# Six edits to a one-core image kernel: three B banks in stage 1, early folds and sums, new banks for a step's last groups, and GpSimd adding the scaled output onto Y

## What is computed

```python
# layer 0: 4x4 mean pooling, two small attentions over the channels, bilinear upsampling, added to x
# layer 1: a Mamba block along one axis, 16 states, then a layernorm, added to x
def step(h, inps):
    dt_t, B_t, C_t, u_t = inps
    dA = jnp.exp(dt_t[..., None] * A)
    h = h * dA + dt_t[..., None] * B_t[:, None, :] * u_t[..., None]
    y = jnp.einsum('bds,bs->bd', h, C_t)
    return (h, y)
# layers 2 and 3: a Mamba-2 block along one axis, then along the other, twice each (8 calls),
# each with its projection added onto its input
scores = jnp.einsum('bln,bsn->bls', Cm, Bm)[..., None] * decay * dt[:, None, :, :]
y = _ssd(xh, dt, A, Bm, Cm) + rev(_ssd(rev(xh), rev(dt), A, rev(Bm), rev(Cm)))
y = _rmsnorm(y.reshape(b, l, DIN) * jax.nn.silu(z), gn_w)
```

## Time and profile before

| | us |
|---|---|
| median of 3 runs | 2561.96 |
| lowest and highest | 2560.93, 2566.42 |
| the profiled execution | 2571.92 |
| its span | 2570.1 |
| stage 0 | 0 to 126 |
| stage 1 | 126 to 863 |
| layernorm, folds, groupnorm | 863 to 910 |
| calls 0 to 3 | 910 to 1712 |
| X takes Y, groupnorm | 1712 to 1730 |
| calls 4 to 7 | 1730 to 2547 |
| the way out | 2547 to 2570 |

### The profile page before, as it was taken

How to read it: one execution, slowest core, us unless ns; L and a number is a source line. 1 busy time by engine, 2 the same in 40 slices (tenths; PEclk the granted TensorE clock), 3 DMA queues, 4 the chain that set the end, 5 groups by cost and what they waited for, 6 DMA issues and landing times.

```text
span 2570.1 us, 58820 instructions
## 1 busy us (share of the span) xinstructions
PE 1997.4 (78%) x24262; PEld 1009.7 (39%) x24262; DVE 1767.8 (69%) x2499; ACT 1666.5 (65%) x2730; POOL 1004.7 (39%) x794
## 2 busy tenths in 40 slices
PE   3257767676776569969969969967997997996996
PEld 3112222222222225535525535533553553553553
DVE  2578888888888867757666765666766665765664
ACT  1166767666676457857857757855875775775774
POOL 0034444444444505506515524522551550651452
PEclk6578888888788879989979989978989998997997
DMA  4000000000000011112112111102102201211111
GB/s 155 0 0 1 0 0 1 1 0 1 1 1 0 1 51 41 26 54 46 29 54 46 29 47 42 40 13 63 38 17 63 46 20 54 46 29 41 39 37 34
DMA packets 95516, 77.48 MB, mean 30 GB/s; under 512 B 65936, under 2 KB 74128, under 8 KB 94736
## 3 DMA queue, kind: packets, MB, share of 16 engines
q1 hardware_dynamic: 91984, 73.32, 11.4%
q10 hardware_dynamic: 3264, 0.39, 0.1%
HBM read 27.02 MB, written 11.53 MB: 15 GB/s over the span
## 4 chain that ended last, share of the span: by engine, by line
PE 52%; DVE 23%; ACT 15%; issue 7%; POOL 1%; DMA 1%; ACTq 0%; DVEq 0%; SPq 0%; POOLq 0%
PE bank L583 11%; PE bank L652 7%; PE bank L615 6%; PE bank L664 6%; DVE Z L1202 6%; PE bank L596 5%; PE bank L672 4%; ACT bank L917 3%; PE bank L511 2%; PE bank L567 2%; DVE XP L1310 2%; DVE SS L1194 2%; ACT bank L814 1%; ACT SQ L885 1%; PE bank L470 1%
## 5 line engine op out<-in xcount | busy, mean ns | idle before, releaser
L992 POOL TENSOR_TENSOR SQ<-SQ,folded_weights 128x512 f32<-128x512 f32 x192 | 243.8, 1271 | 833.0 <-DVE SQ L1426 833.0
L968 POOL TENSOR_TENSOR Y<-Z 128x512 f32<-128x512 f32 x256 | 330.8, 1292 | 528.4 <-DVE Z L1202 299.0
L998 POOL TENSOR_TENSOR SQ<-O,SQ 128x512 f32<-128x512 f32 x208 | 272.6, 1312 | 100.1 <-ACT O L913 71.8
L1202 DVE TENSOR_TENSOR_SCAN Z<-bank,SS 128x512 f32<-128x512 f32 x256 | 310.9, 1215 | 0.5
L511 PE MATMUL bank<-Y,constants 128*128 128x512 f32 x512 | 292.9, 656 | 7.0 <-DVE bank L1210 5.3
L583 PE MATMUL bank<-folded_weights,work 128*64 128x128 f32 x4096 | 295.7, 290 | 0.0
L615 PE MATMUL bank<-SS,work 32*128 32x512 bf16 x1024 | 210.2, 390 | 72.8 <-ACT bank L917 45.7
L583 PEld LDWEIGHTS bank<-folded_weights,work 128*64 128x64 f32 x4096 | 232.9, 143 | 79.5 <-issue 79.5
L652 PE MATMUL bank<-SQ,work 128*32 128x64 f32 x8192 | 256.2, 226 | 0.6
L1363 DVE SCALAR_TENSOR_TENSOR work<-SQ,bank 64x512 f32<-64x512 f32 x256 | 175.4, 685 | 109.1 <-ACT SQ L885 107.1
L1194 DVE TENSOR_TENSOR SS<-SS,bank 128x512 f32<-128x512 f32 x256 | 173.6, 683 | 81.8 <-PE bank L499 65.9
(11 more groups left out here) (260 smaller groups left out, 3734.8 us busy)
## 6 DMA issues: line engine op xcount, KB each, us to landing
work<-XP SPq DMA_DIRECT2D x256, 134.0 KB, 2.4
decays_kept<-extra SPq DMA_DIRECT2D x24, 384.0 KB, 2.3
SS<-decays_kept SPq DMA_DIRECT2D x256, 24.0 KB
block_weights<-callw SPq DMA_DIRECT2D x8, 735.0 KB, 4.3
work<-decays_kept SPq DMA_DIRECT2D x240, 24.0 KB
Z<-state_sel SPq DMA_DIRECT2D x1, 2048.0 KB, 13.1
out<-O SPq DMA_DIRECT2D x2, 1024.0 KB, 8.5
constants<-consts SPq DMA_DIRECT2D x1, 1451.5 KB, 6.3
```

The source lines that it names most:

```text
L968: g.tensor_tensor(hc[t_ % 4], hs[t_ % 4], c_copy[t_ % 4], ALU.mult).then_inc(sg("s1_hc"), 1)
L992: g.tensor_tensor(MM[u % 3], MM[u % 3], Dhalf, ALU.add).then_inc(sg("mixed"), 1)
L998: g.tensor_tensor(MM[u % 3].rearrange("p (h l) -> p h l", l=L), DK[u % 3].rearrange("p (h l) -> p h l", l=L), GM[(u // 8) % 2][:, 64 * (u ...
L1202: v.tensor_tensor_scan(hs[t_ % 4], bank[2 + t_ % 2], dbu[t_ % 2], 0.0, ALU.mult, ALU.add).then_inc(sg("s1_h"), 1)
```

## The change

- **Stage 1.** B goes to banks 4, 5 and 2 in turn and C to banks 6 and 3, both for state t+3 in slot t, one slot earlier in PE's order. weigh writes its product back into B's bank, and the scan reads it there. So B's bank is free once scan(t) is done (s1_h), and PE waits for that. The decays move from banks 2 and 3 to SBUF (decay1).
- **Early folds.** The folds of call 0 and the setup of stage 1 (negA, winx, selBC) are written behind L1038 in stage 0, ahead of the wait for PE's pooling.
- **Sums.** The additions onto X (stage 0, layernorm, first leave) write the column sum as well, and three of the four sums L1015 go.
- **Upsampling.** The three phases go into one operation each: 10 instead of 30, on the same elements.
- **Tables.** groupnorm loads ACT's Ln-and-Exp table before it waits, and ACT takes negA's exponential behind groupnorm(0).
- **Block steps.** GpSimd does grow: groups 0 to 5 ahead of u = 20, 28, ..., 60 and groups 6 and 7 after u = 63. sum_squares(6), project_out(6), project_out(7) and sum_squares(7) stand behind y(63) in PE's order. Group 6 projects into bank 0, group 7 is summed in bank 1 and has a gate buffer of its own.

```diff
+        decay1 = [SS[:, 3072 + 512 * i:3584 + 512 * i] for i in range(2)]
...
-        def every(tau, period, offset, count, last=None):
-            if last is not None and tau == last:
-                return count - 1
+        def every(tau, period, offset, count, moved=()):
+            for i, at in moved:
+                if tau == at:
+                    return i
             i, r = divmod(tau - offset, period)
-            return i if r == 0 and 0 <= i < count - (last is not None) else None
-        LAST, FIRST = L + 6, -9
+            return i if r == 0 and 0 <= i < count - len(moved) else None
+        LAST, FIRST = L + 4, -9
...
-            return 7 if g < NGROUP - 1 else 6
+            return {6: 0, 7: 6}.get(g, 7)
+        def sum_bank(g):
+            return 1 if g == 7 else 7
+        def gate_of(g):
+            return O[:, 2560:3072] if g == 7 else gate
...
-        RH, RC = 4, 4
+        B_BANKS, C_BANKS = (4, 5, 2), (6, 3)
...
-                    tb, ta = t + 2, t - 3
+                    tb, ta = t + 3, t - 3
                     if tb < NK1 * S1:
                         part = parts[(tb // S1) % 2][0:96, :]
                         if tb % S1 == 0:
                             pe.wait_ge(sg("s1_split"), tb // S1 + 1)
                             pe.wait_ge(sg("s1_split_mid"), tb // S1 + 1)
+                        if tb >= 3:
+                            pe.wait_ge(sg("s1_h"), tb - 2)
+                        one = 128 * (tb % S1)
+                        mm(bank[B_BANKS[tb % 3]], selBC[0:96, one:one + 128], part, start=True, stop=True).then_inc(
+                            sg("s1_B"), 1)
                         if tb >= 2:
-                            pe.wait_ge(sg("s1_dbu"), tb - 1)
-                        one = 128 * (tb % S1)
-                        mm(bank[4 + tb % 2], selBC[0:96, one:one + 128], part, start=True, stop=True).then_inc(
-                            sg("s1_B"), 1)
-                        if tb >= 1:
-                            pe.wait_ge(sg("s1_c_copied"), tb)
-                        mm(bank[6], selBC[0:96, 2048 + one:2176 + one], part, start=True, stop=True).then_inc(
+                            pe.wait_ge(sg("s1_c_copied"), tb - 1)
+                        mm(bank[C_BANKS[tb % 2]], selBC[0:96, 2048 + one:2176 + one], part, start=True, stop=True).then_inc(
...
-                    if g < NGROUP - 1:
+                    if out_bank(g) == sum_bank(g):
...
-                    for offset, work_, last_at in ((16, project_out, L + 2), (-7, project_bc, None)):
-                        g = every(tau, 8, offset, NGROUP, last_at)
+                    for offset, work_, moved in ((16, project_out, ()), (-7, project_bc, ())):
+                        g = every(tau, 8, offset, NGROUP, moved)
+                        if work_ == project_out and g is not None and g > 5:
+                            g = None
...
-                    for offset, work_, last_at in ((-3, scores, None), (14, sum_squares, L + 3)):
-                        g = every(tau, 8, offset, NGROUP, last_at)
+                    for offset, work_, moved in ((-3, scores, ()), (14, sum_squares, ((6, L), (7, L + 1)))):
+                        g = every(tau, 8, offset, NGROUP, moved)
+                        if g == 7 and work_ == sum_squares:
+                            project_out(7)
                         if g is not None:
                             work_(g)
+                        if g == 6 and work_ == sum_squares:
+                            project_out(6)
...
+                nc.scalar.preload_act_table_set(LN_EXP)
...
-                    g = every(tau, 8, 14, NGROUP, L + 2)
-                    if g is not None and g < NGROUP - 1:
+                    g = every(tau, 8, 14, NGROUP)
+                    if g is not None:
                         nc.scalar.preload_act_table_set(LN_EXP)
-                    g = every(tau, 8, 15, NGROUP, L + 4)
+                    g = every(tau, 8, 15, NGROUP, ((6, L + 2), (7, L + 3)))
                     if g is not None:
                         act.wait_ge(sg("squares_psum"), c * 8 + g + 1)
-                        A(gate, bank[7], ACT.Ln, bias=C("eps6x4")).then_inc(sg("gate_log"), 1)
+                        A(gate_of(g), bank[sum_bank(g)], ACT.Ln, bias=C("eps6x4")).then_inc(sg("gate_log"), 1)
                         act.wait_ge(sg("gate_log"), c * 8 + g + 1)
-                        A(gate, gate, ACT.Exp, scale=-0.5).then_inc(sg("gate_scale"), 1)
+                        A(gate_of(g), gate_of(g), ACT.Exp, scale=-0.5).then_inc(sg("gate_scale"), 1)
...
+                def grow(k):
+                    pool.wait_ge(sg("scaled"), c * 8 + k + 1)
+                    yq = group_of(Y3, d, k)
+                    g.tensor_tensor(yq, yq, grid(grown), ALU.add).then_inc(sg("grown"), 1)
                 for u in range(L):
+                    if u >= 20 and (u - 20) % 8 == 0:
+                        grow((u - 20) // 8)
...
+                grow(6)
+                grow(7)
...
-                v.tensor_reduce(small[:, 0:1], X, AX.X, ALU.add).then_inc(sg("gn_sum"), 1)
+                if g == 0:
+                    v.tensor_reduce(small[:, 0:1], X, AX.X, ALU.add).then_inc(sg("gn_sum"), 1)
...
+            for piece in range(8):
+                fold(0, piece)
+            dve.wait_ge(sg("stage1_weights_loaded"), 32)
+            negA, early = small[:, 32:48], Order(dve, "s1_setup")
+            v.tensor_scalar(negA, W1("alog"), 80.0, None, ALU.min).then_inc(sg("s1_alog"), 1)
+            dve.wait_ge(sg("s1_expA"), 1)
+            early(v.tensor_scalar(negA, negA, -1.0, None, ALU.mult))
+            early(v.tensor_tensor(W1("winx_b"), W1("winx_a"), W1("wcb"), ALU.mult))
+            early(v.tensor_tensor(W1("winx_a"), W1("winx_a"), W1("wca"), ALU.mult))
+            v.tensor_copy(selBC, stateS).then_inc(sg("s1_selectors"), 1)
...
+                d_ = D5[:, :, :, k].unsqueeze(3).broadcast_to([128, L, 3, b - a])
+                z_ = Z5[:, :, :, k].unsqueeze(3).broadcast_to([128, L, 3, b - a])
+                w_ = wy[:, :, a:b].unsqueeze(1).broadcast_to([128, L, 3, b - a])
+                order(v.tensor_tensor(up[:, :, :, a:b], d_, w_, ALU.mult))
+                order(v.tensor_tensor(up[:, :, :, a:b], up[:, :, :, a:b], z_, ALU.add))
...
-            order(v.tensor_tensor(X, X, O, ALU.add))
+            v.scalar_tensor_tensor(X, X, 1.0, O, ALU.mult, ALU.add, accum_out=small[:, 0:1]).then_inc(sg("gn_sum"), 1)
...
-            v.memset(bank[2], 0.0)
-            v.memset(bank[3], 0.0).then_inc(sg("s1_cleared"), 1)
-            order(v.tensor_scalar(hb, W1("bconv"), 0.5, None, ALU.mult))
+            v.memset(decay1[0], 0.0)
+            v.memset(decay1[1], 0.0).then_inc(sg("s1_cleared"), 1)
...
-                if t_ >= 2:
-                    dve.wait_ge(sg("s1_h"), t_ - 1)
                 if t_ % S1 == 0:
                     dve.wait_ge(sg("s1dt_ready"), t_ // S1 + 1)
-                v.tensor_tensor(dbu[t_ % 2], dtu, bank[4 + t_ % 2], ALU.mult).then_inc(sg("s1_dbu"), 1)
+                v.tensor_tensor(bank[B_BANKS[t_ % 3]], dtu, bank[B_BANKS[t_ % 3]], ALU.mult).then_inc(sg("s1_dbu"), 1)
...
-                v.tensor_tensor_scan(hs[t_ % 4], bank[2 + t_ % 2], dbu[t_ % 2], 0.0, ALU.mult, ALU.add).then_inc(
+                v.tensor_tensor_scan(hs[t_ % 4], decay1[t_ % 2], bank[B_BANKS[t_ % 3]], 0.0, ALU.mult, ALU.add).then_inc(
...
-                order(v.scalar_tensor_tensor(X[:, at], O[:, at], W1("beta"), X[:, at], ALU.add, ALU.add))
+                order(v.scalar_tensor_tensor(X[:, at], O[:, at], W1("beta"), X[:, at], ALU.add, ALU.add,
+                                              accum_out=small[:, 20 + ch:21 + ch]))
+            v.tensor_reduce(small[:, 0:1], small[:, 20:28], AX.X, ALU.add).then_inc(sg("gn_sum"), 1)
...
-                    v.tensor_tensor(grown, bank[out_bank(g)], gate, ALU.mult).then_inc(sg("scaled"), 1)
-                def grow(g):
-                    dve.wait_ge(sg("scaled"), c * 8 + g + 1)
-                    yq = group_of(Y3, d, g)
-                    v.tensor_tensor(yq, yq, grid(grown), ALU.add).then_inc(sg("grown"), 1)
...
-                    for offset, work_, last_at in ((-3, gate_x, None), (6, gate_y, L + 1)):
-                        k = every(tau, 4, offset, 16, last_at)
+                    for offset, work_, moved in ((-3, gate_x, ()), (6, gate_y, ((15, L + 1),))):
...
-                    for offset, work_, last_at in ((17, scale_out, L + 5), (18, grow, L + 5), (-4, gate_bc, None),
-                                                   (-2, scale_scores, None)):
-                        g = every(tau, 8, offset, NGROUP, last_at)
+                    ends = ((6, L + 2), (7, L + 3))
+                    for offset, work_, moved in ((17, scale_out, ends), (-4, gate_bc, ()),
+                                                 (-2, scale_scores, ())):
...
-                v.tensor_tensor(X, X, Y, ALU.add).then_inc(sg("x_added"), 1)
```

(8 more changed lines are left out.)

117 lines of the change are left out of this document (53 added, 64 removed).

## The result

The changed kernel took 2498.93 us in the median of 4 runs (2498.31 to 2499.67), the kernel before 2561.44 beside it. The ratio is 0.9754, 95% interval 0.9737 to 0.9771. That is 62.5 us faster, where 25 were predicted, and outside the predicted range of 2508 to 2560. The profiled execution of the changed kernel took 2498.3 us, that of before 2571.9, so by the two traces the gain is 74 us: 10 of them are the amount by which the trace of before lies above its own median.

A forecast was written before the change was run, and what follows sets the result against it. Stage 1 was taken as bound by DVE, the steady block steps by PE. Gains of 16.0 + 16.7 - 14.5 + 7 = 25 us off the median 2562.0 gave 2537 us, range 2508 to 2560.

The forecast's parts named there:

- Stage 1, the failed step: Stage 1: gain at slot 0 and loss at slot 4 nearly cancel; with the clock, the stage loses 14.5 us.
- C's second bank and the product in place: Stage 1: products in PSUM instead of SBUF taken at nothing; C's second bank got no term.
- The lookahead of B and the clock at slot 4: Stage 1: read-out 1.3 us earlier, L1166 0.7 us later per period, 10.5 us lost; slow clock at slot 4 costs 4 more.
- rival A: Stage 1: the store's delay does not reach L1166, so the third bank gains 20 to 28 us; about 2498, chance 0.14.
- Rival B: Stage 1: PE at 1.2 GHz at slot 4 in every period, 40 us in place of 4; 2573, chance 0.08.
- Rival C: Calls: strided GpSimd additions over 3.6 us hold PE back; at 5 us each 34 us, 2571, chance 0.04.
- Stage 0: Stage 0: tables 3.8, setup 3.7, upsampling 4.1 and sum 4.4 us, together 16.0 us gained.
- Before call 0: Before call 0: folds 9.2 and sum 4.4 us go, scaling beside GpSimd's casts costs 1.0; 12.4 us gained.
- Decays in SBUF: Stage 1: decays in SBUF instead of PSUM taken at nothing, as a scan still has one operand on each side.
- The calls: Block steps: GpSimd's additions shorten PE's wait at each call's end, net 0.9 x 8 = 7 us gained.
- The claim that the order of the last groups matters: End of a call: y(62) and y(63) first, then four groups of products; PE ends about 1.4 us sooner per call.
- GpSimd's addition: Block steps: an addition on GpSimd takes 1.3 us for rows and 1.5 for columns, between 1.3 and 2.4, covered before u = 20.

The follow-up runs named there:

- c_one: The changed kernel with C in bank 6 alone, still for state t+3: 2511.39 us, ratio 0.978.
- before_dbu3: The kernel before with weigh's product in three SBUF buffers, not two, so it waits for the scan of t-3: 2546.9 us, ratio 0.994.
- b_two_ahead: The changed kernel with B of t+2 in slot t, not t+3, in the same three banks: 2498.06 us, ratio 0.9719.
- c_two: The kernel before with C's second bank alone (banks 6 and 3, still t+2), decays in SBUF, product still in SBUF: 2607.08 us, ratio 1.0173.
- calls_before: The changed kernel with all block-step edits undone (additions on VectorE, old order and banks of the last groups): 2514.66 us, ratio 0.9821.
- old_tail: The changed kernel with banks and order of a call's last two groups as before, additions still on GpSimd: 2500.75 us, ratio 0.9749.
- b_three: The kernel before with the third B bank alone, product in B's bank, decays in SBUF, scan wait kept, C still t+2: 2652.87 us, ratio 1.035.

## Why the prediction was wrong

**Stage 1, the failed step.** The sum had +14.5 us, the traces have -15.6, a difference of 30.1. The step that failed is that the prediction moved B and nothing else: it took a steady slot at 1.92 us before and after, without a test, and everything beside B's lookahead and the clock behind it at nothing. A steady slot takes 1.72 us in the changed kernel. The difference splits by the runs, each term a difference of whole stages. They were taken in this order, and another order would split it otherwise (C's second bank is worth 20 us in c_one, beside B of t+3).
- *The edit that it did not price.* The change drops weigh's wait for the scan directly ahead. The diff shows it, the prediction follows the third bank and not this line. before_dbu3 puts 16.0 us on it.
- *C's second bank and the product in place*, taken at nothing: between before_dbu3 (721.8) and b_two_ahead (715.7) lie 6.1 us.
- *The lookahead of B and the clock at slot 4*, "15 x 0.7 = 10.5 us lost" and 4 more: from b_two_ahead to the changed kernel it is 6.5 for both, 8.0 less. Sign and mechanism of the lookahead were right. In the means slot 0 gained 1.84 where the sum had 1.3, slot 4 cost 2.17 where it had 2.0. But the loss does not come back in each of 15 periods: in the late ones the two are equal, and the 6.5 us come mostly from the first two.

16.0 + 6.1 + 8.0 = 30.1. The clock by itself went the other way from the forecast. The front product of slot 4 took 1.91 us in two of 15 periods after, where it took 1.91 in four and 1.73 in one before, and 1.02 in all others. A slow slot 4 lengthened the way to slot 6 by 1.7 us in both kernels (9.4 against 7.7, 11.4 against 9.7), not by 2.7.

That rival A's 2498 lies next to the measured time is luck: its reason was that the delay of the store would not reach L1237, and it did (2.5 us per period). Rival B's 40 us leaves out that five periods had 1.9 us of it already. By the forecast's own terms, 10 x 2.7 + 5 x 0.9 = 31.5, it is some 2564 and not 2573. Rival C's threshold of 3.6 us should be 3.0 (1001.02 - 996.7 - 1.3), which changes nothing at 1.66.

**Stage 0** is right to 0.1 us, and so are its terms (the upsampling 10.4 us, the scaling's wait 5.04, reading the sum 0.08). **Before call 0**: the scaling beside GpSimd's casts took 2.54 us, 0.13 more and not 1.0, and the layernorm's products ran at full clock, 7.13 us instead of 8.83. The 0.8 us that the squares lost beside the casts were not in the sum. **Decays in SBUF** "at nothing" was right for the scan (1.21 us after, 1.22 before), which keeps one operand in PSUM. c_two, where it does not, has a stage 47 us longer. **The calls**: 7 predicted, 11 by the difference, 14.6 by the two traces of calls_before and the changed kernel, which differ by less than traces with equal block steps do. The waits of L1445 shrank as said (2.1 to 0.6, 1.7 to 0.9), and the clock at the call's end did not stay up (3.35 us for the first four products in call 0, against 3.78). Where the rest of the gain comes from is not shown. The claim that the order of the last groups matters fell (old_tail). **GpSimd's addition** takes 1.66 us for columns and 1.27 for rows. Its timeline in calls 0 and 1 of the changed kernel, for the earlier trace rows:

```profile
951.65 1.66 POOL L1011 TENSOR_TENSOR Y<-Y,O 128x512 f32<-128x512 f32 x1
...
1150.66 1.27 POOL L1011 TENSOR_TENSOR Y<-Y,O 128x512 f32<-128x512 f32 x1
```

I had taken 1.5 between 1.3 and 2.4. The Trainium skill's page "GPSIMD Engine Reference", section "Performance pitfalls for Q7 kernels", has half as much again for reads at a step of over 8 bytes. Here it is three tenths more, with one of the two inputs and the result at such a step.

## What to carry to other kernels

When a change gives a ring one more buffer, look first at which waits the code drops with it: here a wait for the instruction directly ahead on the same engine made the next one start 0.19 us later each time, though no data came later. Count an extra slot of lookahead together with what then stands behind its wait in the queue, and move that work ahead of it. A saving of this kind shows in full only on the engine that bounds the stage, so remove the periodic waits first and price it again. Look at the periods one by one and not only at their mean: a price per period times the number of periods was wrong here for the lookahead and for the wait alike, since four kernels settled at the same period.

## What the runs showed of the hardware

- A VectorE product that waits for the scan directly ahead starts 1.31 us after that scan's start, without the wait 1.13.
- A VectorE instruction with all inputs in SBUF slowed beside a GpSimd multiplication: the scan from 1.22 to 1.72 us (c_two), and in b_three the bf16 difference of slot 8 from 0.65 to 1.74. GpSimd stayed at 1.27. In the rows of c_two above, GpSimd had started first.
- Where VectorE had started first, GpSimd paid: beside the scaling of 4096 columns, which took 2.54 us instead of 2.41, a cast took 2.66 instead of 0.61.
- A scalar_tensor_tensor with a column sum beside it took as long as the addition without (4.42 us for 4096 columns, 0.75 for 512), and the sum was read in 0.08.
- The folds took 9.2 us beside GpSimd's casts and 4.9 alone.
- Four kernels with different waits and banks settled at the same period, 44.37 to 44.38 us. Why is open.
